# Two of the four copies that free the attention accumulator move from VectorE to ScalarE

## Chip, cores and metric

One Trainium2 chip, 8 cores, one batch element of 8 on each; the cores share nothing. The metric is the device time in microseconds of the slowest core.

## What is computed

One transformer layer, post-norm, for each batch element: a sequence of S = 4096 rows of 1024. Attention with 16 heads of 64 columns from a compressed latent, then a 1024x1024 layer with weights rounded to 4 bits and a rank 16 addition.

```python
c_kv = h @ W_dkv + b_dkv;  c_q = h @ W_dq + b_dq
k = [c_kv @ W_uk | rotary(h @ W_kr)];  v = c_kv @ W_uv
q = [c_q @ W_uq | rotary(c_q @ W_qr)]
attn = softmax(q k^T / 8)                      # 16 heads, 4096 x 4096
x = layernorm(h + (attn @ v) @ W_o + b_o)
w = simulate_quantize_int4(kernel)
out = layernorm(x + x @ w + bias + (x @ a) @ b)
```

## The kernel before, in words

The program is recorded by helpers, one for each kind of operation (`mm` L237, `tr` L243, `act` L249, `tt` L254, `ts` L260, `red` L272, `cp` L276, `recip` L280), so most rows of the profile carry a helper's line and are told apart by their tiles. Every engine works strictly in the order in which its operations were recorded, and waits on counting semaphores: `sPE`, `sAC`, `sDV` count finished operations of TensorE, ScalarE and VectorE, the `q...` ones count DMAs.

Setup (to about 460 us) projects keys and values for the whole sequence into SBUF and prepares the weights. Then comes the attention, in a loop over 8 query tiles (`qt`, 512 queries), 8 head pairs (`p`) and 32 key chunks (`kc`, 128 keys): 64 pairs of 32 chunks. For each chunk:

- `emit_S`: two matmuls, scores of the two heads, into PSUM banks 0 and 1 or 2 and 3, alternating. It waits for the exponential two chunks back.
- `emit_exp`: one ScalarE operation on 128x1024, into one of four buffers (three in `Psb`, one in `wkr_sb`, hence the two names in the profile).
- `emit_pv`, two chunks late: two matmuls of the probabilities with V (`Vsb`), accumulating over the 32 chunks in banks 4 and 5, columns 2048 to 3071 of `PS`. V has a 65th column of ones for each head, so partition 64 of the result holds the softmax denominators and partitions 0 to 63 the sums.

Banks 4 and 5 are there once. So the first PV matmul of a pair (kc = 0) waits until the results of the pair before have been copied out, which `ep_start` does. It is recorded at kc = 1 of the next pair, right behind the last PV matmul of the old one, and issues four copies on VectorE: the two denominator rows to `bcast_sb` (partitions 0 and 32), the two blocks of sums to `oun_sb`. `dnev` and `oune` keep the semaphore values. TensorE's order there is: scores of chunk 1, last PV of the old pair, scores of chunk 2, first PV of the new pair (which waits), scores of chunk 3. ScalarE's is: exponentials of chunks 1, 2, 3.

`ep_chain_gen` carries on while the next pair runs: it writes the denominators to DRAM (`rden`) and reads them back broadcast to all partitions (POOL's queue), takes the reciprocal (L280, 128x512) and multiplies `oun_sb` by it on VectorE (chunk 8), and issues the result to `o_dram` from ScalarE's queue (chunk 13), where the issue waits for the multiply and the exponentials stand behind it.

Beside that, `tail_gen` does the output projection, both layer norms and the last layer of the tile before, a few operations for each chunk from kc = 3 on, on TensorE (bank 7), VectorE (`tA`, `h2`, `x1T`, `st`, `stv`) and a little on ScalarE; `qbuild_gen` builds the next tile's queries. In the first query tile there is no tail work.

Of the kernel before, what the change touches and what calls it, by code (L numbers as in the profile page):

```python
# [9 lines left out]
AF = mybir.ActivationFunctionType  # L10
# [111 lines left out]
def build_program(S):  # L122
# [59 lines left out]
    bcast_sb = sbt("bcast_sb", [128, 512], F32)  # L182
# [16 lines left out]
    PS = nc.alloc_psum_tensor("PS", [128, 4096], F32)  # L199
# [46 lines left out]
    def act(out, in_, func, waits=(), scale=1.0, bias=0.0, extra=()):  # L246
        return S_.ev("scalar",
                     (lambda e, o=out, i=in_, f=func, sc=scale, b=bias:
                      e.activation(o, i, f, scale=sc, bias=b)),  # L249
                     waits, [("sAC", 1)] + list(extra))  # L250
# [24 lines left out]
    def cp(out, in_, waits=(), extra=()):  # L275
        return S_.ev("vector", (lambda e, o=out, i=in_: e.tensor_copy(o, i)),  # L276
                     waits, [("sDV", 1)] + list(extra))
# [21 lines left out]
    for nm, dst in (("ident", ident_sb), ("bdkv", bdkv_sb),  # L299
# [9 lines left out]
                     sem="qCVa")["qCVa"])  # L309
    qcv["dq"] = ("qCVb", dma("gpsimd", wdq_sb,  # L310
                    dr["W_dq"].rearrange("(c p) n -> p c n", p=128),
                    sem="qCVb")["qCVb"])
# [3 lines left out]
                    sem="qCVc")["qCVc"])  # L316
# [10 lines left out]
    for half in range(2):  # L327
# [5 lines left out]
            sem="qWsc")  # L333
# [96 lines left out]
    for s in range(NSP):  # L430
        tau = 512 * s
        tl = dma("sync", cos_sb[:, :], dr["cosT"][:, tau:tau + 512], sem="qT",
                 waits=([("sDV", tbl_free)] if tbl_free else []))
# [4 lines left out]
        for i in range(4):  # L438
            par = i % 2
            w = [("sPE", hload_seen[par])] if hload_seen[par] else []  # L440
            if hload_gate[par]:
# [4 lines left out]
                     waits=w)  # L446
            ldv = ld[qH[par]]
            for c in range(8):
                bk = 2 * par + c // 4
                w2 = []  # L450
                if c == 0:
# [5 lines left out]
                    elif s > 0:  # L457
# [3 lines left out]
                          waits=w2)  # L461
                if c == 3 or c == 7:
                    dst = hT[:, 0:4096].rearrange("p (c t) -> p c t", t=512)[
                        :, 4 * (c // 4):4 * (c // 4) + 4, 128 * i:128 * (i + 1)]
                    e = act(dst, PS[:, 512 * bk:512 * (bk + 1)].rearrange(
                                "p (c t) -> p c t", t=128),
                            AF.Copy, waits=[("sPE", last["sPE"])])
# [5 lines left out]
        for c in range(8):  # L473
            w = []
            if c == 0:
                w = [("sAC", hT_ready)]
# [7 lines left out]
        for c in range(8):  # L484
            mm(PS[:, 2560:3072], wdq_sb[:, 128 * c:128 * (c + 1)],
               hT[:, 512 * c:512 * (c + 1)],
               waits=([qcv["dq"]] if s == 0 and c == 0 else []),
# [3 lines left out]
                 waits=[("sPE", pe_ckv)])  # L491
        ckv_sb = cq_buf[:, 0:512]
        e2 = act(cq_buf[:, 512:1024], PS[:, 2560:3072], AF.Identity, bias=bdq_sb[:, 0:1],
                 waits=[("sPE", pe_cq)] + ([("qCw", cw_cnt)] if cw_cnt else []))
        ckv_ready = e2["sAC"]
        cw = dma("sync", cq_scr[:, tau:tau + 512], cq_buf[:, 512:1024],
                 sem="qCw", waits=[("sAC", e2["sAC"])])
# [3 lines left out]
        for blk, bk in enumerate((6, 7, 0)):  # L501
            for c in range(8):
                w = []
                if c == 0:
                    if blk == 0 and rope_done:
                        w = [("sDV", rope_done)]
                    if blk == 0 and s == 0:
                        w.append(qcv["kr"])
                    if blk == 2:
                        w = [("sAC", ev_done[0])]  # L510
# [7 lines left out]
                 waits=[("sPE", pe_krot - 8)])  # L518
        e5 = act(c0c, PS[:, 0:512], AF.Identity, bias=bkr_sb[:, 2:3],
                 waits=[("sPE", pe_krot)] + ([("qKb", kb_cnt)] if kb_cnt else []))  # L520
        kb1 = dma("sync", rotk_scr[128:256, tau:tau + 512], c0c,
                  sem="qKb", waits=[("sAC", e5["sAC"])])
        e3b = act(c0b_sb[:, :], PS[:, 512 * 6:512 * 7], AF.Identity, bias=bkr_sb[:, 0:1],
                  waits=[("sAC", e4["sAC"])] + ([("qKb", kb_cnt)] if kb_cnt else []))
        e6 = tt(c0b_sb[:, :], c0b_sb[:, :], cos_sb[:, :], ALU.mult,
                waits=[("sAC", e3b["sAC"]), ("qT", tbl_val)])
        e7 = tt(c0s_sb[:, :], c0s_sb[:, :], sin_sb[:, :], ALU.mult,
                waits=[("sDV", e6["sDV"])])
        e8 = tt(c0b_sb[:, :], c0b_sb[:, :], c0s_sb[:, :], ALU.add,
                waits=[("sDV", e7["sDV"])])  # L530
# [3 lines left out]
                  sem="qKb", waits=[("sDV", e8["sDV"])])  # L534
# [4 lines left out]
        for p in range(NP):  # L539
            bk = 1 + p % 2  # L540
            w = []
            if p < 2:
                w = [("sAC", ckv_ready), ("sAC", ev_done[bk])]
                if s == 0:
                    w.append(qcv["kcat"])
            else:
                w = [("sAC", kn_evac[p % 2])]
# [10 lines left out]
        for i in range(4):  # L558
            for half in range(2):
                k = 2 * i + half  # L560
                bk = 3 + k % 2
                if k == 0:
                    w = [("sAC", ev_done[3]), ("sAC", ckv_ready), ("qBB", buv["qBB"])]
# [3 lines left out]
                elif k == 1:  # L567
                    w = [("sAC", e1["sAC"])]
# [120 lines left out]
    denb = [0] * (NGT + 1)  # L689
# [18 lines left out]
    for qt in range(NQT):  # L708
# [3 lines left out]
        def ep_start(PIDX2):  # L712
            lastG = PIDX2 * NKC + NKC - 1
            op_ = 512 * (PIDX2 % 2)
            c1 = cp(bcast_sb[0:1, 0:512], PS[64:65, 2048:2560],
                    waits=[("sPE", denb[lastG])] +
                          ([("sDV", bcf_[PIDX2 - 1])] if PIDX2 > 0 else []))
            c2 = cp(bcast_sb[32:33, 0:512], PS[64:65, 2560:3072])
            dnev[PIDX2] = c2["sDV"]
            cp(oun_sb[0:64, op_:op_ + 512], PS[0:64, 2048:2560],  # L720
               waits=[("qOD", norm_[PIDX2 - 2])] if PIDX2 > 1 else [])
            e = cp(oun_sb[64:128, op_:op_ + 512], PS[0:64, 2560:3072])
            oune[PIDX2] = e["sDV"]
            return e["sDV"], c2["sDV"]

        def ep_chain_gen(PIDX2, e_dv, c2_dv):
            op_ = 512 * (PIDX2 % 2)
            oup = oun_sb[:, op_:op_ + 512]
            Wg = (PIDX2 + 1) * NKC + 1
            def ph(x):  # L730
                return Wg + max(1, (x * NKC) // 32)
            while gctr[0] < ph(2):
                yield "spin"
            wdma0 = dma("gpsimd", rden[PIDX2:PIDX2 + 1, 0:512], bcast_sb[0:1, 0:512],
                        sem="qBC", waits=[("sDV", c2_dv)] +
                        ([("qOD", norm_[PIDX2 - 1])] if PIDX2 > 0 else []))
            wdma = dma("gpsimd", rden[PIDX2:PIDX2 + 1, 512:1024],
                       bcast_sb[32:33, 0:512], sem="qBC")
            rdw[PIDX2] = wdma["qBC"]
            while gctr[0] < ph(4):  # L740
                yield "spin"
            bl = dma("gpsimd", bcast_sb[0:64, :],
                     rden[PIDX2:PIDX2 + 1, 0:512].partition_broadcast(64),
                     sem="qBC", waits=[("qBC", wdma["qBC"])])
            bl2 = dma("gpsimd", bcast_sb[64:128, :],
                      rden[PIDX2:PIDX2 + 1, 512:1024].partition_broadcast(64),
                      sem="qBC")
            while gctr[0] < ph(7):
                yield "spin"
            rr = recip(bcast_sb[:, :], bcast_sb[:, :],  # L750
                       waits=[("qBC", bl2["qBC"]), ("sDV", e_dv)])
            nn = tt(oup, oup, bcast_sb[:, :], ALU.mult,
                    waits=[("sDV", rr["sDV"])])
            bcf_[PIDX2] = nn["sDV"]
            while gctr[0] < ph(12):
                yield "spin"
            od = dma("scalar", o_dram[PIDX2 * 128:(PIDX2 + 1) * 128, :],
                     oup, sem="qOD", waits=[("sDV", nn["sDV"])])
            norm_[PIDX2] = od["qOD"]
# [31 lines left out]
        def emit_pv(p, kc):  # L791
            G = (qt * NP + p) * NKC + kc
            PIDX = qt * NP + p
            p3 = G % 4
            first = (kc == 0)
            lastk = (kc == NKC - 1)
            w = [("sAC", expd[G])]
            if first and PIDX > 0:
                w += [("sDV", oune[PIDX - 1]), ("sDV", dnev[PIDX - 1])]
            mm(PS[0:65, 2048:2560],  # L800
               Vsb[:, 1040 * kc + 65 * (2 * p):1040 * kc + 65 * (2 * p) + 65],
               PSB4[p3][:, 0:512], waits=w,
               start=first, stop=lastk, tp=(0, 0))
            r = mm(PS[0:65, 2560:3072],
                   Vsb[:, 1040 * kc + 65 * (2 * p + 1):1040 * kc + 65 * (2 * p + 1) + 65],
                   PSB4[p3][:, 512:1024],
                   start=first, stop=lastk, tp=(0, 0))
            denb[G] = r["sPE"]
# [337 lines left out]
```

How the kernel before makes its waits and increments, by code:

```python
            def emit(eng):  # L1108
                for fn, waits, incs in S_.events[eng_name]:
                    for s, v in waits:
                        if v > 0:
                            eng.wait_ge(sems[s], v)
                    if fn is None:
                        continue
                    ins = fn(eng)
                    for s, a in incs:
                        ins = ins.then_inc(sems[s], a)
```

## Time and profile before

| | us |
|---|---|
| two runs | 3258.97 and 3322.42, median 3290.7 |
| the profiled execution | 3256.61 |
| its span, slowest core | 3255.0 (cores from 3240.3) |
| TensorE matmul busy | 2555.7 (79%), 10584 matmuls |
| ScalarE busy | 2113.9 (65%) |
| VectorE busy | 1241.5 (38%) |
| GpSimd busy | 230.2 (7%) |
| mean granted TensorE clock, cores | 0.867 to 0.873 |

PE is TensorE, PEld its weight load, ACT is ScalarE, DVE is VectorE, POOL is GpSimd; a q behind a name is that engine's DMA queue. "x2" behind an operation means that so many stand merged in a row of the timeline; the time given is then from the first one's start to the last one's end. In brackets is the idle time before it and what ended it. A granted clock of 1.00 is 2.4 GHz, 0.5 is 1.2 GHz; a value between is a mean over a stretch with both.

### The profile page before, as it was taken

What the parts mean: (1) busy time and instruction counts of PE and PEld (TensorE: products, weight loads), DVE (VectorE), ACT (ScalarE), POOL (GpSimd) and SP (SyncE); (2) the same over time, 40 slices, a digit from 0 to 9 for tenths busy, and PEclk for the clock granted to TensorE, in tenths of its full rate; (3) what the DMA queues carried; (4) which work ended last, traced back from release to release, by engine and by line L of the source; (5) the groups of instructions that cost most, each with busy time, mean ns of one, the idle gap of its engine ahead of it and who ended that gap; (6) DMA issues with size and microseconds to landing.
All of it is one profiled execution on the core that took longest, in us unless ns stands there. A gap on an engine that the chain in (4) does not pass through costs nothing.

```text
span 3255.0 us, 40114 instructions; the slowest of 8 cores (3240.3 to 3255.0 us)
## 1 busy us (share of the span) xinstructions
PE 2555.7 (79%) x10584; PEld 790.4 (24%) x10584; DVE 1241.5 (38%) x1610; ACT 2113.9 (65%) x2353; POOL 230.2 (7%) x393
## 2 busy tenths in 40 slices
PE   3455678899788978888889878898899788988733
PEld 1222212222222222222222222222222222222211
DVE  1456212224443344334432444244433443344344
ACT  1223368888577867786668767886688677877600
POOL 4000000000000010000000000000000000010000
PEclk8666679999898989898889999998899898999866
DMA  6323310001211121212120122012111211121121
GB/s 105 114 94 98 77 57 23 19 24 41 68 56 53 34 81 36 70 34 65 59 67 24 53 66 77 28 43 80 46 58 41 69 54 53 33 77 56 50 91 39
DMA packets 89938, 188.43 MB, mean 58 GB/s; under 512 B 20579, under 2 KB 50532, under 8 KB 89476
## 3 DMA queue, kind: packets, MB, share of 16 engines
q1 hardware_dynamic: 44292, 82.81, 8.5%
q0 software_dynamic: 31616, 77.88, 8.3%
q10 hardware_dynamic: 13824, 25.17, 2.0%
q8 instruction: 107, 1.75, 0.2%
q14 instruction: 99, 0.81, 0.1%
HBM read 144.65 MB, written 51.64 MB: 60 GB/s over the span
## 4 chain that ended last, share of the span: by engine, by line
PE 56%; DVE 17%; issue 10%; ACT 9%; DMA 7%; POOL 1%; DVEq 0%; SPq 0%; ACTq 0%; POOLq 0%
PE PS L237 54%; ACT Psb L249 5%; DVE tA L254 3%; DVE oun_sb L276 3%; ACT wkr_sb L249 2%; DVE bcast_sb L280 2%; PE PS L243 2%; DVE bcast_sb L276 2%; DVE h L254 1%; DVE Qsb L260 1%; DMA rotq_scr<-c0s_sb 1%; DMA x_scr<-tA 1%; DMA h<-h 1%; POOL Vsb L284 1%; DVE Psb L260 1%
## 5 line engine op out<-in xcount | busy, mean ns | idle before, releaser
L249 ACT ACTIVATE Psb<-PS 128x1024 bf16<-128x1024 f32 x1536 | 1514.2, 1042 | 377.7 <-PE PS L237 371.2
L237 PE MATMUL PS<-Psb,Vsb 128*65 128x512 bf16 x3072 | 1026.5, 418 | 184.6 <-DVE oun_sb L276 160.3
L237 PE MATMUL PS<-Qsb,Ksb 64*128 64x512 bf16 x4096 | 842.6, 405 | 68.1 <-ACT Psb L249 45.0
L249 ACT ACTIVATE wkr_sb<-PS 128x1024 bf16<-128x1024 f32 x512 | 534.0, 1043 | 277.3 <-PE PS L237 276.5
L237 PEld LDWEIGHTS PS<-Qsb,Ksb 64*128 64x128 bf16 x4096 | 220.9, 93 | 960.7 <-issue 958.6
L237 PEld LDWEIGHTS PS<-Psb,Vsb 128*65 128x65 bf16 x3072 | 224.0, 114 | 569.4 <-issue 569.4
L237 PE MATMUL PS<-wkr_sb,Vsb 128*65 128x512 bf16 x1024 | 333.9, 409 | 2.6 <-ACT wkr_sb L249 2.6
L254 DVE TENSOR_TENSOR tA<-PS,h 128x512 f32<-128x512 f32 x128 | 88.5, 692 | 585.6 <-PE PS L237 546.4
L280 DVE RECIPROCAL bcast_sb<-bcast_sb 128x512 f32<-128x512 f32 x64 | 214.3, 3349 | 166.7 <-DMA bcast_sb<-rden 166.7
L276 DVE COPY bcast_sb<-PS 1x512 f32<-1x512 f32 x128 | 87.7, 685 | 452.4 <-PE PS L237 449.8
L237 PE MATMUL PS<-wbuf,osb 128*128 128x512 bf16 x512 | 168.4, 415 | 69.6 <-DVE tA L254 53.1
L243 PE MATMUL PS<-ident_sb,h 128*128 128x128 f32 x512 | 104.1, 360 | 113.1 <-DMA h<-h 42.4
L237 PE MATMUL PS<-wbuf,x1T 128*128 128x512 bf16 x512 | 168.0, 422 | 16.0 <-DVE tA L254 13.1
L230 POOL DMA_DIRECT2D rden<-bcast_sb x128 | 63.1, 498 | 1640.9 <-DVE bcast_sb L276 1545.8
L249 ACT ACTIVATE st<-stv,eps_sb 128x1 f32<-128x1 f32 x64 | 19.5, 304 | 190.5 <-DVE stv L254 190.3
L243 PEld LDWEIGHTS PS<-ident_sb,h 128*128 128x128 f32 x512 | 83.5, 189 | 145.5 <-issue 141.8
L260 DVE TENSOR_SCALAR Qsb<-PS,bqc_sb 128x512 bf16<-128x512 f32 x64 | 48.0, 751 | 168.1 <-PE PS L237 168.1
L237 PEld LDWEIGHTS PS<-wkr_sb,Vsb 128*65 128x65 bf16 x1024 | 73.7, 112 | 128.8 <-issue 128.8
L260 DVE TENSOR_SCALAR tA<-tA,stm 128x1024 f32<-128x1024 f32 x64 | 48.2, 753 | 132.7 <-ACT str_ L249 132.7
L249 ACT ACTIVATE Qsb<-PS 128x512 bf16<-128x512 f32 x64 | 37.2, 596 | 90.8 <-PE PS L243 90.5
L237 PE MATMUL PS<-osb,cq_buf 128*128 128x512 bf16 x64 | 36.5, 596 | 72.8 <-DVE Vsb L254 72.5
L276 DVE CAST oun_sb<-PS 64x512 bf16<-64x512 f32 x128 | 87.4, 683 | 4.0
(88 smaller groups left out, 1351.7 us busy)
## 6 DMA issues: line engine op xcount, KB each, us to landing
h<-h SPq DMA_DIRECT2D x64, 512.0 KB, 3.9
wbuf<-wo_p POOLq DMA_DIRECT2D x32, 512.0 KB, 5.8
bcast_sb<-rden POOLq DMA_DIRECT2D x128, 128.0 KB, 2.8
x_scr<-tA POOLq DMA_DIRECT2D x32, 512.0 KB, 3.1
wbuf<-wf_p POOLq DMA_DIRECT2D x32, 512.0 KB, 5.8
h<-x_scr SPq DMA_DIRECT2D x32, 512.0 KB, 3.6
out<-tA ACTq DMA_DIRECT2D x32, 512.0 KB, 2.6
o_dram<-oun_sb ACTq DMA_DIRECT2D x64, 128.0 KB, 1.7
```

Source lines behind the costliest of these rows:

```text
L230: return S_.ev(q, (lambda e, o=out, i=in_: e.dma_start(out=o, in_=i)), waits, [(sem, 16)] + list(extra))
L237: e.matmul(o, l, r, start=s1, stop=s2, tile_position=t, skip_group_check=k)),
L243: (lambda e, o=out, i=in_: e.transpose(o, i, ident_sb[:, :])),
L249: e.activation(o, i, f, scale=sc, bias=b)),
L254: (lambda e, o=out, x=in0, y=in1, p=op: e.tensor_tensor(o, x, y, op=p)),
L260: e.tensor_scalar(o, i, a, None, op0=p)),
L276: return S_.ev("vector", (lambda e, o=out, i=in_: e.tensor_copy(o, i)), waits, [("sDV", 1)] + list(extra))
L280: return S_.ev("vector", (lambda e, o=out, i=in_: e.reciprocal(o, i)), waits, [("sDV", 1)] + list(extra))
L284: return S_.ev("gpsimd", (lambda e, a=ap, x=v: e.memset(a, x)), waits, [("sGP", 1)])
```

## The change

`ep_start` still issues four copies, in another order and on two engines: the two blocks of sums first, on VectorE, the first of them with the wait for the last PV matmul; then the two denominator rows on ScalarE, with the same wait and the one for the multiply of the pair before. The semaphore that `dnev` counts is now `sAC`, and the two places that wait for it follow: the write to `rden` and the first PV matmul.

```diff
         def ep_start(PIDX2):
             lastG = PIDX2 * NKC + NKC - 1
             op_ = 512 * (PIDX2 % 2)
-            c1 = cp(bcast_sb[0:1, 0:512], PS[64:65, 2048:2560],
-                    waits=[("sPE", denb[lastG])] +
-                          ([("sDV", bcf_[PIDX2 - 1])] if PIDX2 > 0 else []))
-            c2 = cp(bcast_sb[32:33, 0:512], PS[64:65, 2560:3072])
-            dnev[PIDX2] = c2["sDV"]
             cp(oun_sb[0:64, op_:op_ + 512], PS[0:64, 2048:2560],
-               waits=[("qOD", norm_[PIDX2 - 2])] if PIDX2 > 1 else [])
+               waits=[("sPE", denb[lastG])] +
+                     ([("qOD", norm_[PIDX2 - 2])] if PIDX2 > 1 else []))
             e = cp(oun_sb[64:128, op_:op_ + 512], PS[0:64, 2560:3072])
             oune[PIDX2] = e["sDV"]
-            return e["sDV"], c2["sDV"]
+            c1 = act(bcast_sb[0:1, 0:512], PS[64:65, 2048:2560], AF.Copy,
+                     waits=[("sPE", denb[lastG])] +
+                           ([("sDV", bcf_[PIDX2 - 1])] if PIDX2 > 0 else []))
+            c2 = act(bcast_sb[32:33, 0:512], PS[64:65, 2560:3072], AF.Copy)
+            dnev[PIDX2] = c2["sAC"]
+            return e["sDV"], c2["sAC"]
...
             wdma0 = dma("gpsimd", rden[PIDX2:PIDX2 + 1, 0:512], bcast_sb[0:1, 0:512],
-                        sem="qBC", waits=[("sDV", c2_dv)] +
+                        sem="qBC", waits=[("sAC", c2_dv)] +
...
             if first and PIDX > 0:
-                w += [("sDV", oune[PIDX - 1]), ("sDV", dnev[PIDX - 1])]
+                w += [("sDV", oune[PIDX - 1]), ("sAC", dnev[PIDX - 1])]
```

ScalarE's order at the first boundary (end of the first pair, first 13 chunks of the second), before. `Psb` and `wkr_sb` are the exponentials' buffers, the last row is the issue of the finished block to DRAM:

```order
L249 ACTIVATE wkr_sb<-PS 128x1024 [waits sPE]
L249 ACTIVATE Psb<-PS 128x1024 [waits sPE] x3
L249 ACTIVATE wkr_sb<-PS 128x1024 [waits sPE]
L249 ACTIVATE Psb<-PS 128x1024 [waits sPE] x3
L249 ACTIVATE wkr_sb<-PS 128x1024 [waits sPE]
L249 ACTIVATE Psb<-PS 128x1024 [waits sPE] x3
L249 ACTIVATE wkr_sb<-PS 128x1024 [waits sPE]
L249 ACTIVATE Psb<-PS 128x1024 [waits sPE] x2
L230 DMA o_dram<-oun_sb 128x512 [waits sDV]
```

The same place now:

```order
L249 ACTIVATE wkr_sb<-PS 128x1024 [waits sPE]
L249 ACTIVATE Psb<-PS 128x1024 [waits sPE] x2
L249 ACTIVATE bcast_sb<-PS 1x512 [waits sPE]
L249 ACTIVATE bcast_sb<-PS 1x512
L249 ACTIVATE Psb<-PS 128x1024 [waits sPE]
L249 ACTIVATE wkr_sb<-PS 128x1024 [waits sPE]
L249 ACTIVATE Psb<-PS 128x1024 [waits sPE] x3
L249 ACTIVATE wkr_sb<-PS 128x1024 [waits sPE]
L249 ACTIVATE Psb<-PS 128x1024 [waits sPE] x3
L249 ACTIVATE wkr_sb<-PS 128x1024 [waits sPE]
L249 ACTIVATE Psb<-PS 128x1024 [waits sPE] x2
L230 DMA o_dram<-oun_sb 128x512 [waits sDV]
```

The two row copies stand between the exponentials of chunks 1 and 2 of the new pair. The issue to `o_dram` keeps its place behind chunk 13.

VectorE's order at the first two boundaries, before:

```order
L260 TENSOR_SCALAR Qsb<-PS,bqc_sb 128x512 [waits sPE] x8
L276 COPY bcast_sb<-PS 1x512 [waits sPE]
L276 COPY bcast_sb<-PS 1x512
L276 CAST oun_sb<-PS 64x512 x2
L280 RECIPROCAL bcast_sb<-bcast_sb 128x512 [waits qBC,sDV]
L254 TENSOR_TENSOR oun_sb<-oun_sb,bcast_sb 128x512 [waits sDV]
L276 COPY bcast_sb<-PS 1x512 [waits sPE,sDV]
```

and now:

```order
L260 TENSOR_SCALAR Qsb<-PS,bqc_sb 128x512 [waits sPE] x8
L276 CAST oun_sb<-PS 64x512 [waits sPE]
L276 CAST oun_sb<-PS 64x512
L280 RECIPROCAL bcast_sb<-bcast_sb 128x512 [waits qBC,sDV]
L254 TENSOR_TENSOR oun_sb<-oun_sb,bcast_sb 128x512 [waits sDV]
L276 CAST oun_sb<-PS 64x512 [waits sPE]
```

The casts follow the wait for TensorE directly. TensorE's order is the same as before, apart from the semaphore that the first PV matmul of a pair waits for; POOL's likewise, for its write to `rden`.

## Rows read from the trace of the kernel before

**Rows 1.** Groups of instructions: busy us, mean ns, idle before, releasers.
```profile
L237 PE MATMUL PS<-Psb,Vsb 128*65 128x512 bf16 x3072 | 1026.5, 418 | 184.6 <-DVE oun_sb L276 160.3 <-DVE st L254 24.2
...
L254 DVE TENSOR_TENSOR tA<-PS,h 128x512 f32<-128x512 f32 x128 | 88.5, 692 | 585.6 <-PE PS L237 546.4 <-DMA x_scr<-tA 39.2
L276 DVE COPY bcast_sb<-PS 1x512 f32<-1x512 f32 x128 | 87.7, 685 | 452.4 <-PE PS L237 449.8
L276 DVE CAST oun_sb<-PS 64x512 bf16<-64x512 f32 x128 | 87.4, 683 | 4.0
```

**Rows 2.** The chain of waits, 496 to 506: start us, us, what.
```profile
497.91 0.68 DVE bcast_sb L276
...
500.75 0.24 issue
501.00 5.02 PE PS L237 x15
```

**Rows 3.** Timeline of the same boundary: start us, us, instruction, [idle before].
```profile
496.48 2.85 ACT L249 ACTIVATE Psb<-PS 128x1024 bf16<-128x1024 f32 x3
496.80 0.39 PE L237 MATMUL PS<-Qsb,Ksb 64*128 64x512 bf16 x2
...
497.67 0.39 PE L237 MATMUL PS<-Qsb,Ksb 64*128 64x512 bf16 x2
...
501.00 0.82 PE L237 MATMUL PS<-Psb,Vsb 128*65 128x512 bf16 x2 [2.94 <-DVE oun_sb L276]
...
502.54 1.02 ACT L249 ACTIVATE wkr_sb<-PS 128x1024 bf16<-128x1024 f32 x1 [3.20 <-PE PS L237]
```

**Rows 4.** Groups of ScalarE, shapes kept apart, columns as in rows 1.
```profile
L249 ACT ACTIVATE Psb<-PS 128x1024 bf16<-128x1024 f32 x1536 | 1514.2, 1042 | 377.7 <-PE PS L237 371.2 <-PE PS L243 3.0 <-issue 0.3
...
L249 ACT ACTIVATE Ksb<-PS,bkc_sb 128x512 bf16<-128x512 f32 x64 | 41.2, 687 | 4.2 <-PE PS L237 3.4
L249 ACT ACTIVATE Qsb<-PS 128x512 bf16<-128x512 f32 x64 | 37.2, 596 | 90.8 <-PE PS L243 90.5
...
L249 ACT ACTIVATE str_<-st 128x1 f32<-128x1 f32 x64 | 13.0, 203 | 6.2 <-ACT st L249 0.4
...
L249 ACT ACT_TABLE_LOAD x1 | 1.3, 1283 | 12.0 <-PE PS L243 12.0
```

**Rows 5.** Timeline at the change from the first to the second query tile.
```profile
704.24 2.85 ACT L249 ACTIVATE Psb<-PS 128x1024 bf16<-128x1024 f32 x3 [1.46 <-PE PS L237]
...
707.77 0.59 PE L237 MATMUL PS<-Psb,Vsb 128*65 128x512 bf16 x2 [1.98 <-DVE oun_sb L276]
```

**Rows 6.** Timeline around the issue of a finished block, first boundary of a query tile.
```profile
1436.42 0.69 DVE L254 TENSOR_TENSOR oun_sb<-oun_sb,bcast_sb 128x512 bf16<-128x512 bf16 x1
...
1438.04 0.33 ACTq L230 DMA_DIRECT2D o_dram<-oun_sb  x1
```

**Rows 7.** Two pairs of equal work: us, busy by engine, PEclk, DMA share, GB/s.
```profile
568.00:600.70 32.70, 29.33 (x131) 8.35 (x129) 6.82 (x7) 29.78 (x33) 2.04 (x4) 1.00 0.05 17
600.70:634.70 34.00, 30.63 (x131) 8.47 (x129) 6.79 (x7) 29.90 (x33) 2.03 (x4) 0.95 0.05 16
```

**Rows 8.** 12 us behind two boundary waits, columns as in rows 7.
```profile
1424.70:1436.70 12.00, 9.06 (x42) 2.57 (x40) 6.37 (x6) 9.24 (x11) 2.03 (x4) 1.00 0.08 24
...
1697.10:1709.10 12.00, 9.07 (x31) 2.04 (x29) 6.28 (x6) 6.87 (x8) 2.04 (x4) 0.72 0.07 24
```

**Rows 9.** Timeline of TensorE behind two shorter waits elsewhere.
```profile
1179.22 0.59 PE L237 MATMUL PS<-wbuf,osb 128*128 128x512 bf16 x2 [1.88 <-DVE tA L254]
...
1180.56 1.06 PE L237 MATMUL PS<-wbuf,osb 128*128 128x512 bf16 x2
...
1534.22 0.38 PE L237 MATMUL PS<-cq_buf,wq_sb 128*128 128x512 bf16 x1 [1.23 <-DVE c0s_sb L260]
...
1534.85 0.62 PE L237 MATMUL PS<-Psb,Vsb 128*65 128x512 bf16 x2
```

**Rows 10.** Who waited for whom, TensorE: us in total, times, longest.
```profile
PE PS L237 <- DVE tA L254: 66.3, 46, 11.2
```

## The prediction

> **What bounds the kernel now.** I read the page first. Its busy times (in the table above) have TensorE at 79% of the span and ScalarE at 65%, so no engine is full, and the question is what the two main engines wait for. The groups of instructions answer it: the matmuls of the probabilities with V lose 184.6 us to waits for VectorE, 160.3 us of it put down to the casts of `oun_sb`, and 24.2 us to an op that stood just behind them [rows 1]. There are 64 head pairs in a core (8 query tiles of 8) and so 63 boundaries; 184.6 / 63 is 2.93 us at each. The chain of waits around one boundary [rows 2] shows how it is made up: the last PV matmul of the old pair ends, then four VectorE copies stand one behind the other from 497.91 to 500.75, and TensorE goes on at 501.00. The timeline there [rows 3] shows both victims. TensorE is idle for 2.94 us. ScalarE, which in this stretch runs its exponentials without a break, runs dry at 499.33 and starts the next at 502.54, after 3.20 us: the scores that it needs are queued behind the waiting PV matmul.
>
> Two regimes matter for what a shorter wait is worth. Between boundaries without tail work ScalarE sets the pace: three exponentials take 2.85 us with the last 1.03 long, so one starts every 0.91 us; the TensorE group of scores and PV starts every 0.87 us (496.80 to 497.67) [rows 3]. With tail work TensorE is the fuller one. In both an earlier first PV matmul moves everything behind it.
>
> **The change, part by part.** VectorE loses 128 copies of a 1x512 row (685 ns each, two and two casts between 497.91 and 500.75, a start every 0.72 us) [rows 1, 2]. It keeps two casts, which now wait for the last PV matmul themselves. They would stand from 497.91 to 499.31, and with the 0.25 us from the end of a cast to the PV matmul (500.75 to 501.00 [rows 2]) TensorE could go on at 499.56.
>
> ScalarE gains the 128 row copies, and its order puts them behind the exponential of chunk 1 and ahead of that of chunk 2. The three exponentials of [rows 3] are chunks 0, 1 and 2, so the first row copy takes the place of the third, at 496.48 + 2 x 0.91 = 498.30. No row shows ScalarE copying a 1x512 row. Its shortest op, 128x1, takes 203 ns; 128x512 out of PSUM takes 596 ns without a bias and 687 ns with one [rows 4]. VectorE's copy of one row costs as much as its cast of 64 rows (685 against 683 ns [rows 1]), so rows don't count but columns do, and I take 596. The next starts after 0.46 us (0.91 less the 0.45 us that separate 1042 from 596). Copies at 498.30 and 498.76, end 499.36, TensorE at 499.61. With 203 ns the casts would decide (499.56), with 687 ns it would be 499.70 to 499.80: between 1.2 and 1.44 us saved, and I take 501.00 - 499.61 = 1.39.
>
> The exponential of chunk 2 moves from 498.30 to 499.22 and ends at 500.25. It is first needed by the scores of chunk 4, which reuse its bank and start a group and more after 499.61 + 0.55 (the scores of chunk 3) + 0.87, at about 501.0, so the 0.92 us on ScalarE are hidden. ScalarE's next one, chunk 3, follows the first PV matmul and moves with it, so the 1.39 us reach the exponentials too. The cover would be gone if ScalarE had no idle stretch there; it stood 3.20 us [rows 3].
>
> At the seven changes of query tile the wait is 1.98 us only, because the exponentials start late there: three from 704.24 [rows 5]. The row copies would start at 706.06 and end at 707.12, TensorE goes on at 707.37 instead of 707.77, and 0.40 us are saved. The sum of the waits is 56 x 1.39 + 7 x 0.40 = 80.6 us. Setup and the last tail are left as they are.
>
> What is late next: the issue of `o_dram<-oun_sb` stands in ScalarE's order ahead of chunk 14 and waits for the multiply by the reciprocals. That multiply ends at 1437.11, the issue is at 1438.04: 0.93 us to spare [rows 6]. The time of the multiply doesn't come from TensorE but from the trip of the denominators through DRAM, whose start stays within 0.1 us, since the second row copy ends at 499.36 instead of 499.31. With 1.39 us less ahead of it, ScalarE would stand 0.5 us, its exponentials behind. This holds at about 15 boundaries, those of the first query tile and the first of each later one, where tail work does not delay ScalarE: 8 us back. The POOL queue only changes which semaphore it waits for.
>
> **The clock.** The granted clock is the second term. In pairs with the same work, 568.0 to 600.7 and 600.7 to 634.7, the time is 32.7 us at 1.00 and 34.0 us at 0.95 [rows 7]. A mean of 0.95 over 34 us means 3.4 us at the lower level, 1.2 GHz, and they cost 1.3 us, 0.4 us for each. The lower level comes right after a boundary wait, but not behind each: two stretches of 12 us behind the same 2.94 us wait have 1.00 and 0.72 [rows 8]. Summed over the stretches of 12 us behind all 63 boundaries I count 243 us at the lower level: 129 at the 40 whose pair number in the tile is 0, 1, 3, 4 or 6, 77 at numbers 2 and 5, where VectorE is late and the wait mostly 3.2 to 3.5 us, and 37 at number 7. The first kind's wait shrinks to 1.55 us, the second's to about 2.0. Is that short enough? A wait of 1.88 us is followed by PV and projection matmuls of double length within a microsecond and a half; one of 1.23 us, by none [rows 9]. 1.55 lies between. I credit three quarters of the 129 and a quarter of the 77: 116 us x 0.4 = 46 us. The bounds are 0 and 243 x 0.4 = 97 us.
>
> [...]
>
> **Sum.** 80.6 + 46 - 8 = 118.6 us. The profiled execution took 3256.6 us (its span 3255.0 and 1.6 around it), so 3138 us. The median of the two runs shown, 3290.7, lies between 3258.97 and 3322.42; the profiled one agrees with the lower. About 2%, 65 us, is what a measurement of this kernel tells from no change.
>
> **Rivals.** (a) The clock doesn't follow: 1.55 us is still long enough beside the other small gaps. Then 80.6 - 8 is left: 3184 us. For it: 1.88 us is followed by double lengths. Chance 0.18.
>
> (b) VectorE's later work gives it back: in the tiles with tail work TensorE also waits 66.3 us for `tA` [rows 10], which stands behind the 3.35 us reciprocal. If these chains keep their place in time at pair numbers 2, 4 and 5, 24 x 1.39 = 33 us and their share of the clock, some 20 us, are lost: 3191 us. Against it: VectorE loses 1.43 us of work ahead of them, and the `tA` additions with which these chains begin wait 546.4 us for TensorE [rows 1], so they come earlier when it does. Chance 0.14.
>
> (c) Slower: switching from Exp to Copy and back reloads ScalarE's function table. A load takes 1283 ns [rows 4]. With one ahead of the row copies and one behind, ScalarE is taken from 498.30 for 2 x 1.28 + 0.92 = 3.48 us; chunk 2's exponential starts at 501.78 and chunk 3's can't before 502.69, where it would have been 502.1 at the full clock (501.00 and 0.55 + 0.32 + 0.25 behind it). From 2.9 us of ScalarE work on the change loses; here 0.6 us x 56 = 33 us: 3290 us. Against it: the one load of the program covers Copy, Identity, Abs, Ln and Exp alike. Chance 0.03. A slow read is a weaker form of it: row copies and casts read the same two PSUM banks at once, in other partitions, which no row of this trace shows. The Trainium skill, page PSUM — Partial Sum Buffer, section on bank collisions, says that two engines may access one bank together as long as they are in different 32-partition quadrants, and row 64 is in another than rows 0 to 63.
>
> (d) The wait doesn't go, because something else stood just behind the copies: 3250 us. The chain [rows 2] names nothing. Chance 0.03.
>
> **Numbers.** The forecast, 3138 us, has 0.62, with a range of its own of 3100 to 3170. The range for 8 in 10 runs from 3085 (the whole clock term) to 3212 (a and b together, nearly). Faster by over 2% is everything below 3191: 0.62, nearly all of (a) and half of (b), 0.86; within 2%: 0.11; slower by over 2%: 0.03, for (c) with a longer load.
>
> **What would show it.** In the profile after: VectorE's chain at a boundary of 1.40 us; row copies on ScalarE of about 600 ns directly behind chunk 1's exponential; the idle time before the first PV matmul at 1.5 to 1.6 us and 63 such waits at some 104 us instead of 184.6; ScalarE idle before `o_dram<-oun_sb` or the exponential behind it at about 15 places; PEclk of 1.00 behind most boundaries and a mean above 0.90 over the run. Row copies of over 1 us, table loads, or an unchanged clock would make the forecast wrong, in that order of weight.

## The result

The changed kernel takes 0.9717 of the time before, with a 95% interval of 0.968 to 0.9753: faster. The median of its 11 runs is 3177.17 us (3160.47 to 3268.92), that of 10 runs of the kernel before 3265.49 us; both hold some runs in which one die ran at a lower clock, which the ratio leaves out, and so do all the ratios below. The profiled execution took 3162.96 us against 3256.61, 93.65 us less; 118.6 us less were forecast.

The groups of instructions of the changed kernel (columns as in [rows 1]):

```profile
L237 PE MATMUL PS<-Psb,Vsb 128*65 128x512 bf16 x3072 | 996.4, 407 | 111.5 <-ACT bcast_sb L249 98.1 <-DVE st L254 13.4
...
L280 DVE RECIPROCAL bcast_sb<-bcast_sb 128x512 f32<-128x512 f32 x64 | 214.4, 3351 | 263.6 <-DMA bcast_sb<-rden 263.6
...
L276 DVE CAST oun_sb<-PS 64x512 bf16<-64x512 f32 x128 | 87.3, 682 | 421.4 <-PE PS L237 419.3
L249 ACT ACTIVATE bcast_sb<-PS 1x512 f32<-1x512 f32 x128 | 75.5, 590 | 4.0 <-PE PS L237 0.9
```

The first line answers to the first of [rows 1]: the waits before a pair's first PV matmul fell from 184.6 to 111.5 us, and most of them (98.1 us) now end with ScalarE's row copy. The row copies take 590 ns each. The table load is in the profile once, as before. VectorE's reciprocal now waits 263.6 us for its DMA, where it waited 166.7 us before.

The timeline of one boundary (the same as in [rows 3]; TensorE's weight loads left out):

```profile
502.42 1.02 ACT L249 ACTIVATE Psb<-PS 128x1024 bf16<-128x1024 f32 x1
502.69 0.39 PE L237 MATMUL PS<-Qsb,Ksb 64*128 64x512 bf16 x2
502.87 1.40 DVE L276 CAST oun_sb<-PS 64x512 bf16<-64x512 f32 x2 [18.69 <-PE PS L237]
503.46 1.20 ACT L249 ACTIVATE bcast_sb<-PS 1x512 f32<-1x512 f32 x2
504.69 1.02 ACT L249 ACTIVATE Psb<-PS 128x1024 bf16<-128x1024 f32 x1
504.81 0.59 PE L237 MATMUL PS<-Psb,Vsb 128*65 128x512 bf16 x2 [1.73 <-ACT bcast_sb L249]
```

The two engines work side by side. VectorE is done at 504.27, ScalarE at 504.66, so ScalarE's pair decides; TensorE starts 0.15 us later, and its wait is 1.73 us where it was 2.94. ScalarE no longer runs dry: its next exponential follows at once.

Behind it the clock still falls at some boundaries and not at others, as the windows view shows for 12 us behind the second and the third (columns as in [rows 7]):

```profile
503.50:515.50 12.00, 10.69 (x42) 2.75 (x42) 4.49 (x4) 10.73 (x13) 2.04 (x4) 0.86 0.08 24
536.00:548.00 12.00, 10.49 (x47) 3.07 (x47) 4.66 (x4) 11.68 (x14) 2.03 (x4) 1.00 0.07 24
```

Counted in the clock records of the traces, the 12 us behind a boundary hold time at the lower level at 409 of the 504 boundaries of the eight cores before (254 us on a core, median) and at 224 of them now (109 us).

To see where the time went, the span is cut where the first copies at a boundary start and where those behind the last pair start. The windows view of the attention phase between them, slowest core, before and after (same columns):

```profile
464.20:3079.90 2615.70, 2252.61 (x9544) 662.91 (x9542) 986.82 (x1233) 1965.75 (x2127) 181.61 (x350) 0.92 0.16 51
```

```profile
471.40:2990.60 2519.20, 2195.80 (x9544) 658.14 (x9542) 899.32 (x1106) 2044.38 (x2253) 182.89 (x350) 0.95 0.17 53
```

VectorE lost 87 us of work, ScalarE gained 79, and the clock rose from 0.92 to 0.95. The same cut on all eight cores gives the medians that are used from here on ("low clock" is the time at the lower level in this phase, "PV wait" the idle time before the PV matmuls in the whole run):

| us, median of 8 cores | setup | attention | last tail | low clock | PV wait |
|---|---|---|---|---|---|
| before | 465.0 | 2609.8 | 175.2 | 421.5 | 187.2 |
| after | 463.7 | 2517.6 | 170.5 | 286.7 | 114.4 |
| difference | -1.3 | -92.2 | -4.7 | -134.8 | -72.8 |

Not all that was saved arrived. TensorE's other waits grew: its scores matmuls wait for exponentials 81.9 us in the attention phase instead of 59.7, and the x @ a matmuls 24.7 us for `x1T` instead of 21.4. By place, 11.8 of the first 22 us are at chunk 19 of pair number 2 of the tiles (15.3 us after, 3.5 before), 4.1 at chunk 16, 2.8 at chunk 14 of pair number 5 and 2.6 at chunk 7 of pair number 6. The place in pair number 2 can be read in the timelines. VectorE before, then after:

```profile
1126.93 3.35 DVE L280 RECIPROCAL bcast_sb<-bcast_sb 128x512 f32<-128x512 f32 x1 [1.18 <-DMA bcast_sb<-rden]
1130.38 0.69 DVE L254 TENSOR_TENSOR oun_sb<-oun_sb,bcast_sb 128x512 bf16<-128x512 bf16 x1
1131.63 0.69 DVE L254 TENSOR_TENSOR tA<-PS,h 128x512 f32<-128x512 f32 x1 [0.56 <-PE PS L237]
```

```profile
1103.87 3.35 DVE L280 RECIPROCAL bcast_sb<-bcast_sb 128x512 f32<-128x512 f32 x1 [3.88 <-DMA bcast_sb<-rden]
1107.32 0.69 DVE L254 TENSOR_TENSOR oun_sb<-oun_sb,bcast_sb 128x512 bf16<-128x512 bf16 x1
1107.93 0.69 DVE L254 TENSOR_TENSOR tA<-PS,h 128x512 f32<-128x512 f32 x1
...
1114.34 0.16 DVE L254 TENSOR_TENSOR stv<-stv,st 128x1 f32<-128x1 f32 x1 [0.17 <-DVE st L254]
```

The addition to `tA` used to wait 0.56 us for TensorE. Now TensorE is earlier, and the addition comes straight behind the multiply: the reciprocal, held by its DMA, sets the pace of the layer norm chain. ScalarE then waits for the end of that chain, and TensorE waits for ScalarE (changed kernel):

```profile
1114.59 0.29 ACT L249 ACTIVATE st<-stv,eps_sb 128x1 f32<-128x1 f32 x1 [1.51 <-DVE stv L254]
...
1116.29 0.39 PE L237 MATMUL PS<-Qsb,Ksb 64*128 64x512 bf16 x2 [2.12 <-ACT Psb L249]
```

Before, that scores matmul waited 0.50 us. Pair number 2 takes 39.8 us where it took 39.1, while the other seven got shorter by 0.9 to 3.0 us.

### The profile page after: what moved, and what is told of

Read it like the earlier page. It is cut to its first block, busy times and chain, and to the rows that moved or that the text cites. A ratio compares the mean times of both kernels' runs of the same rounds, so it can differ in the third digit from the quotient of the medians.

```text
span 3161.4 us, 40178 instructions; the slowest of 8 cores (3145.2 to 3161.4 us)
## 1 busy us (share of the span) xinstructions
PE 2493.6 (79%) x10584; PEld 787.5 (25%) x10584; DVE 1150.9 (36%) x1482; ACT 2193.9 (69%) x2481; POOL 231.4 (7%) x393
## 4 chain that ended last, share of the span: by engine, by line
PE 54%; DVE 14%; ACT 10%; issue 10%; DMA 9%; POOL 1%; DVEq 1%; SPq 0%; ACTq 0%; POOLq 0%
PE PS L237 52%; ACT Psb L249 5%; DVE tA L254 4%; DVE bcast_sb L280 3%; ACT bcast_sb L249 2%; PE PS L243 2%; ACT wkr_sb L249 2%; DVE h L254 2%; DMA bcast_sb<-rden 1%; DMA h<-h 1%; DMA x_scr<-tA 1%; DMA rotq_scr<-c0s_sb 1%; DVE Psb L260 1%; DVE Qsb L260 1%; POOL Vsb L284 1%
## 5 line engine op out<-in xcount | busy, mean ns | idle before, releaser
L237 PE MATMUL PS<-Psb,Vsb 128*65 128x512 bf16 x3072 | 996.4, 407 | 111.5 <-ACT bcast_sb L249 98.1
L237 PE MATMUL PS<-Qsb,Ksb 64*128 64x512 bf16 x4096 | 828.0, 398 | 93.4 <-ACT Psb L249 68.9
L280 DVE RECIPROCAL bcast_sb<-bcast_sb 128x512 f32<-128x512 f32 x64 | 214.4, 3351 | 263.6 <-DMA bcast_sb<-rden 263.6
L237 PE MATMUL PS<-wbuf,x1T 128*128 128x512 bf16 x512 | 158.8, 402 | 14.8 <-DVE tA L254 12.4
L237 PEld LDWEIGHTS PS<-wbuf,osb 128*128 128x128 bf16 x512 | 53.6, 105 | 144.0 <-issue 97.5
```

The lines of the kernel that those rows point to most:

```text
L237: e.matmul(o, l, r, start=s1, stop=s2, tile_position=t, skip_group_check=k)),
L280: return S_.ev("vector", (lambda e, o=out, i=in_: e.reciprocal(o, i)), waits, [("sDV", 1)] + list(extra))
```

## The experiments

**First question: how much of the gain is the shorter wait, how much the clock?** The six or eleven added matmuls below fill TensorE's wait and write a bank that is free then; the results are not used, everything else is computed as before.

e4, on the kernel before:

```diff
             if first and PIDX > 0:
+                for k_ in range(11):
+                    mm(PS[:, 3072:3584], wq_sb[:, 0:128], Vsb[:, 0:512],
+                       waits=[("sDV", qb_state["qb_bank_free"])] if k_ == 0 else [])
                 w += [("sDV", oune[PIDX - 1]), ("sDV", dnev[PIDX - 1])]
```

> The kernel before with 11 such matmuls ahead of each pair's first PV matmul, where it stands 2.94 us; its copies and their wait are as before. This isolates the clock. If the clock term of 0.4 us per us at the lower clock is right, the time at the lower clock in the attention phase falls from 421 us to about 200 and the time by some 80 us, to about 3180, a ratio of 0.975. If only the shorter wait counted in the change, it stays at 3257 within 10 us.

Measured: ratio 0.9681 (0.9637 to 0.9726) to the kernel before. The low clock falls from 421.5 to 146.8 us, the attention phase from 2609.8 to 2517.5. A boundary in its timeline (eight of the eleven stand in the stretch shown):

```profile
505.70 1.89 PE L237 MATMUL PS<-Vsb,wq_sb 128*128 128x512 bf16 x8
506.40 1.40 DVE L276 CAST oun_sb<-PS 64x512 bf16<-64x512 f32 x2
...
508.05 0.59 PE L237 MATMUL PS<-Psb,Vsb 128*65 128x512 bf16 x2 [0.46 <-DVE oun_sb L276]
...
509.14 1.02 ACT L249 ACTIVATE wkr_sb<-PS 128x1024 bf16<-128x1024 f32 x1 [2.76 <-PE PS L237]
```

The PV matmul still comes when the last cast is done, and ScalarE still runs dry for 2.76 us. Only what TensorE does in the wait is different, and behind it the clock:

```profile
505.20:517.20 12.00, 11.54 (x52) 3.59 (x51) 5.36 (x5) 9.24 (x11) 2.03 (x4) 1.00 0.08 24
```

Behind none of the 63 boundaries, on any core, is there time at the lower level left within 12 us; the 146.8 us lie elsewhere. So the clock term is shown, and its price: 92.3 us for 274.7 us at the lower level, 0.34 us for each. The forecast had used 0.4.

e3, the same on the changed kernel with six:

```diff
             if first and PIDX > 0:
+                for k_ in range(6):
+                    mm(PS[:, 3072:3584], wq_sb[:, 0:128], Vsb[:, 0:512],
+                       waits=[("sDV", qb_state["qb_bank_free"])] if k_ == 0 else [])
                 w += [("sDV", oune[PIDX - 1]), ("sAC", dnev[PIDX - 1])]
```

> The changed kernel with 6 more matmuls (128x512, result unused, bank 6) in TensorE's order ahead of each pair's first PV matmul, where TensorE stands 1.73 us; at the full clock they take 1.3 us and fit in. Theory (clock term): the time at the lower clock in the attention phase falls from 287 us (median of the cores) to about 200, and at 0.4 us for each the time falls by about 35 us against the changed kernel. Rival (the lower clock is not tied to these waits or costs nothing, since ScalarE paces): no gain, or a loss of up to 10 us where the six run at the lower clock and end late.

Measured: 0.9588 (0.9551 to 0.9625); low clock 187.7 us, attention phase 2487.2, 30.4 us less than in the changed kernel for 99.0 us, 0.31 us for each. The gain decides for the clock. Behind the second and the third boundary of e3:

```profile
502.70:514.70 12.00, 11.67 (x54) 3.50 (x53) 4.77 (x4) 11.73 (x15) 2.04 (x4) 1.00 0.08 24
535.50:547.50 12.00, 11.56 (x51) 3.30 (x51) 4.04 (x2) 11.72 (x14) 2.03 (x4) 1.00 0.08 23
```

The lower level is gone behind 497 of the 504 boundaries. So the changed kernel's waits of 1.73 us were still long enough to bring the clock down at nearly half of its boundaries.

**Second: is it the second engine or the new order?** e10 puts the row copies back on VectorE, behind the casts:

```diff
-            c1 = act(bcast_sb[0:1, 0:512], PS[64:65, 2048:2560], AF.Copy,
-                     waits=[("sPE", denb[lastG])] +
-                           ([("sDV", bcf_[PIDX2 - 1])] if PIDX2 > 0 else []))
-            c2 = act(bcast_sb[32:33, 0:512], PS[64:65, 2560:3072], AF.Copy)
-            dnev[PIDX2] = c2["sAC"]
+            c1 = cp(bcast_sb[0:1, 0:512], PS[64:65, 2048:2560],
+                    waits=[("sDV", bcf_[PIDX2 - 1])] if PIDX2 > 0 else [])
+            c2 = cp(bcast_sb[32:33, 0:512], PS[64:65, 2560:3072])
+            dnev[PIDX2] = c2["sDV"]
```

> The changed kernel with the two row copies put back on VectorE, behind the casts: the change's order without its second engine. Theory (the gain comes from copies side by side): the wait before a first PV matmul is 2.9 us again, 187 us in all, the lower clock in the attention phase above 400 us, and the time is that of the kernel before or some 5 to 15 us more, since the denominators start 1.4 us later on their way. Rival (the order matters, casts first): part of the 97 us stays.

Measured: 1.0016 (0.9988 to 1.0043), without the 5 to 15 us more that I had thought possible; PV wait 178.3 us, low clock 426.7. The PV matmuls wait for VectorE's row copies again:

```profile
L237 PE MATMUL PS<-Psb,Vsb 128*65 128x512 bf16 x3072 | 1025.7, 418 | 175.7 <-DVE bcast_sb L276 175.6
```

The order alone is worth nothing; the gain is the second engine's. One detail helps below: with the denominators written 1.4 us later and TensorE no earlier, the wait at chunk 19 of pair number 2 is 7.4 us, twice that of the kernel before, with no row copy on ScalarE.

**Third: what took part of the gain back?** The forecast had named one place, the issue of the finished block on ScalarE's queue. e1 moves it from chunk 13 to 19:

```diff
-            while gctr[0] < ph(12):
+            while gctr[0] < ph(18):
                 yield "spin"
             od = dma("scalar", o_dram[PIDX2 * 128:(PIDX2 + 1) * 128, :],
```

> The changed kernel with one number changed: the issue of the finished block on ScalarE's queue moves from chunk 13 to chunk 19. Theory A (the gain was cut because ScalarE stands at this issue for VectorE's multiply): the waits of the scores matmuls for the exponentials fall from 82 us in the attention phase back to about 60, and the time falls by 12 to 22 us against the changed kernel (ratio to it about 0.994). Theory B (the cut comes from the 1.2 us of row copies in ScalarE's stream itself): these waits stay near 80 us and the time within 5 us of the changed kernel.

Measured: 0.9496 (0.9451 to 0.9541), attention phase 2458.2 us, 59 us below the changed kernel. Neither theory holds: the scores' waits did not fall (85.9 us), and the gain is three times what A promised. The edit does two things. `tail_gen` starts when `norm_` is set, and that moved too, so all the tail's work stands at later chunks. e6 separates them; it sets the mark where it was:

```diff
             while gctr[0] < ph(12):
                 yield "spin"
+            norm_[PIDX2] = V("qOD") + 16
+            while gctr[0] < ph(18):
+                yield "spin"
             od = dma("scalar", o_dram[PIDX2 * 128:(PIDX2 + 1) * 128, :],
```

> The changed kernel with the issue of the finished block at chunk 19, as in e1, but with the tail's work recorded at the very chunks where it was. Theory (e1's gain of some 57 us against the changed kernel came from the tail's work starting six chunks later, not from the issue): here only the 4 us of waits at chunk 16 go, so the time is that of the changed kernel, 0 to 8 us below. Rival (the issue itself held everything up): the same gain as e1, some 57 us, ratio to the kernel before 0.950.

Measured: 0.9671 (0.965 to 0.9691), attention phase 2513.1 us, 4.5 below the changed kernel; the wait at chunk 16 is gone. The issue costs 4 to 5 us, which is too little for the ratios of whole runs to tell: their intervals overlap. e8 is the edit of e1 on the kernel before:

```diff
-            while gctr[0] < ph(12):
+            while gctr[0] < ph(18):
```

> The kernel before with the edit of e1 (issue at chunk 19, which also lets the tail's work start six chunks later). If e1's gain is one of the tail's place, it shows without the change too: 40 to 60 us below the kernel before, ratio 0.982 to 0.988, with pair number 3 near 45 us instead of 56. If it belongs to the change (the issue made late by the shorter wait), the time stays within 5 us of the kernel before, which had 0.85 us and more to spare at that issue.

Measured: 0.9734 (0.9681 to 0.9788). The edit, which moves the issue and the tail's work, is worth 84 us in the attention phase (2609.8 to 2526.1) without any of the change, more than I expected; pair number 3 falls from 56.2 to 44.6 us, and pair number 7 takes over work (38.1 to 44.2). Pair number 3, before and then in e8:

```profile
1156.20:1212.90 56.70, 42.18 (x170) 12.21 (x170) 25.39 (x38) 32.66 (x37) 5.81 (x11) 0.85 0.30 92
```

```profile
1141.70:1186.90 45.20, 37.63 (x156) 10.93 (x156) 25.39 (x32) 31.23 (x35) 4.74 (x9) 0.92 0.25 79
```

It holds 14 matmuls less, and the query building in it no longer meets the layer norm: the 30.8 us wait for `stv` is 0 in e1 and e8. So e1's gain is no property of the change. With e6's 4 to 5 us for the issue, the place of the tail's work is what it comes from.

e2 adds to e1 the reciprocal at chunk 11 instead of 8:

```diff
-            while gctr[0] < ph(7):
+            while gctr[0] < ph(10):
                 yield "spin"
             rr = recip(bcast_sb[:, :], bcast_sb[:, :],
```

> As e1, and the reciprocal recorded at chunk 11 in place of chunk 8. Theory C (VectorE, standing 7 us for the denominators' way through DRAM with the tail's work behind it, passes the wait on to TensorE and ScalarE): VectorE's wait for this DMA falls from 264 us to under 120, and the time falls by another 5 to 15 us below e1. Rival: that wait is hidden; then the time is that of e1 within 5 us, or a little more, since the multiply comes later.

Measured: 0.9454 (0.941 to 0.9498), attention phase 13.7 us below e1, as expected in size. Its reason was not: VectorE's wait for this DMA fell only from 215.0 us in e1 to 191.8. e7 has the reciprocal at chunk 11 with the tail unmoved:

```diff
-            while gctr[0] < ph(7):
+            while gctr[0] < ph(10):
...
+            norm_[PIDX2] = V("qOD") + 16
+            while gctr[0] < ph(18):
+                yield "spin"
```

> As e6, and the reciprocal recorded at chunk 11 in place of 8, the tail's work unmoved. Theory (in pair number 2 of a tile the layer norm chain stands on VectorE behind a reciprocal that waits for its DMA, and ScalarE's Ln stands for the chain): the scores' wait at chunk 19 of pair number 2, 15 us in all, falls to under 4, pair number 2 gets shorter by 1.5 us, and the time is 8 to 15 us below e6, unless the later reciprocal meets another chain. Rival (that wait comes from the row copies on ScalarE): it stays at 15 us.

Measured: 0.9515 (0.9491 to 0.9539), attention phase 2456.5, 57 us below e6. And the named wait went the wrong way, from 14.1 to 24.1 us. The timeline of VectorE in pair number 2 shows what stands there:

```profile
1090.00 1.22 DVE L254 TENSOR_TENSOR tA<-tA,bbuf 128x1024 f32<-128x1024 f32 x1 [0.17 <-DVE tA L254]
1091.14 3.34 DVE L280 RECIPROCAL bcast_sb<-bcast_sb 128x512 f32<-128x512 f32 x1
1094.59 0.69 DVE L254 TENSOR_TENSOR oun_sb<-oun_sb,bcast_sb 128x512 bf16<-128x512 bf16 x1
1095.20 1.21 DVE L272 TENSOR_REDUCE st<-tA 128x1 f32<-128x1024 f32 x1
```

At chunk 11 the reciprocal falls into the middle of the layer norm chain, with 4 us of its own, and TensorE's scores waited 3.44 us there. The gain came from elsewhere: the waits at chunk 14 of pair number 5 (32.0 to 4.6 us) and for `x1T` (25.1 to 0), partly replaced by 17.6 us of transposes waiting for `x1T`. So the reciprocal's place had made that wait at chunk 14 too, most of which (29 us) is in the kernel before already. The miss still left two makers for the wait of pair number 2, the reciprocal and the row copies. e11 takes the reciprocal out of the chain's way altogether:

```diff
-            while gctr[0] < ph(7):
+            while gctr[0] < ph(12):
+                yield "spin"
+            norm_[PIDX2] = V("qOD") + 16
+            while gctr[0] < ph(19):
                 yield "spin"
             rr = recip(bcast_sb[:, :], bcast_sb[:, :],
...
-            while gctr[0] < ph(12):
+            while gctr[0] < ph(22):
                 yield "spin"
             od = dma("scalar", o_dram[PIDX2 * 128:(PIDX2 + 1) * 128, :],
```

> The changed kernel with the tail's work unmoved, the reciprocal at chunk 20 and the issue at chunk 23, so that neither stands ahead of the layer norm chain that ends in ScalarE's Ln at about chunk 17 of pair number 2. Theory: the scores' wait at chunk 19 of pair number 2 (15 us after the change, 24 us in e7) falls to under 4 us, since only VectorE's reciprocal made it; pair number 2 falls from 39.8 to about 38 us. Rival (ScalarE's row copies made it): it stays near 15 us. The whole time should be below e6; where it lands depends on which chains the reciprocal meets at chunk 20, and I expect 3110 to 3160.

Measured: 0.9732 (0.9709 to 0.9755). At that place (e11's timeline):

```profile
1130.38 0.39 PE L237 MATMUL PS<-Qsb,Ksb 64*128 64x512 bf16 x2 [0.48 <-ACT Psb L249]
...
1130.91 3.35 DVE L280 RECIPROCAL bcast_sb<-bcast_sb 128x512 f32<-128x512 f32 x1
```

The wait is 3.3 us in all, as in the kernel before (3.5), and pair number 2 takes 37.2 us, with the row copies still on ScalarE. The reciprocal made it. The whole is not faster than the changed kernel (the expected 3110 to 3160 us were missed). With the reciprocal at chunk 20 the scores' waits at chunk 29 of pair numbers 1 and 6 are 43 us, where they were 9, and the wait for `stv` rises from 30.7 to 54.5. That the reciprocal meets other chains there is the likely reason; it was not tested.

**The parts together.** e9 is e2 with the six matmuls of e3:

```diff
+                for k_ in range(6):
+                    mm(PS[:, 3072:3584], wq_sb[:, 0:128], Vsb[:, 0:512],
+                       waits=[("sDV", qb_state["qb_bank_free"])] if k_ == 0 else [])
...
-            while gctr[0] < ph(7):
+            while gctr[0] < ph(10):
...
-            while gctr[0] < ph(12):
+            while gctr[0] < ph(18):
```

> e2 (issue at chunk 19 and reciprocal at chunk 11, tail later) with e3's six filler matmuls. If the clock term adds to the others, some 25 to 30 us below e2: about 3067, ratio to the kernel before 0.938. If ScalarE paces e2 so far that the clock is hidden, less than 10 us below e2.

Measured: 3037.77 us, ratio 0.9298 (0.9278 to 0.9318), faster than both kernels; low clock 99.0 us, attention phase 2395.0, 49.5 us below e2 for 160.4 us less at the lower clock: 0.31 us for each again. More than expected: in e2 the lower clock stood behind 335 of the 504 boundaries, 167 us on a core in the 12 us behind them, where the changed kernel with nearly the same waits (114.4 us in all, 112.5 in e2) has 224 and 109 us. In e9 it is behind none. So the length of the wait does not decide alone.

| median of 8 cores, us | ratio to before | attention | low clock | PV wait |
|---|---|---|---|---|
| before | 1 | 2609.8 | 421.5 | 187.2 |
| after | 0.9717 | 2517.6 | 286.7 | 114.4 |
| e1 issue late, tail late | 0.9496 | 2458.2 | 259.4 | 112.5 |
| e2 and reciprocal late | 0.9454 | 2444.5 | 259.4 | 112.5 |
| e3 filler, after | 0.9588 | 2487.2 | 187.7 | 25.5 |
| e4 filler, before | 0.9681 | 2517.5 | 146.8 | 34.4 |
| e6 issue late | 0.9671 | 2513.1 | 291.8 | 114.4 |
| e7 issue and reciprocal late | 0.9515 | 2456.5 | 252.6 | 114.4 |
| e8 e1's edit, before | 0.9734 | 2526.1 | 332.8 | 175.2 |
| e9 e2 and filler | 0.9298 | 2395.0 | 99.0 | 24.3 |
| e10 order only | 1.0016 | 2612.9 | 426.7 | 178.3 |
| e11 reciprocal at 20 | 0.9732 | 2532.4 | 290.1 | 114.4 |

## Why the prediction was right, and where not

The measured time lies in the range: the median, 3177 us, is 39 us above the forecast of 3138, the profiled execution, 3163 us, 25 us above it. Its steps:

- **The shorter wait, 80.6 us: right in kind, 10% too high.** 72.8 us measured. The step that was off is "the next starts after 0.46 us". The row copies do not overlap as the exponentials do: the first starts when the exponential has ended (503.46), not 0.91 us after its start, and they start 0.61 us apart. So ScalarE was done 1.79 us after the first cast's start and not 1.45, TensorE followed after 0.15 us and not 0.25, and 1.21 us of waiting were saved in place of 1.39. The 596 ns for one of them was right (590).
- **The clock, 46 us: right in sum, by two errors.** The low clock fell by 134.8 us, not 116 (some 145 us less in the 12 us behind the boundaries, 10 to 20 more elsewhere), and one us of it is worth 0.31 to 0.34 us, not 0.4; at 0.33 that is 44.5 us. The price had come from one pair of pairs [rows 7]. e4 shows that this term is real and not a companion of the shorter wait. Rival (a), without it, was wrong, though what spoke for it holds in part: the wait became 1.73 us and not 1.55, and behind it one stretch still has 0.86 where the next has 1.00. The sign "a mean above 0.90 over the run" did not come (0.881 to 0.889), nor could it by the forecast's own 116 us, which lift the mean from 0.87 to 0.89 only.
- **What is late next, 8 us at the issue of the finished block: right in place, too high.** The idle time there is real, 4 to 5 us by e6 and by the waits at chunk 16.
- **Rival (b), priced at 53 us and left out of the forecast: where the sum was wrong.** "They come earlier when TensorE does" holds for most chains, but not for the one in pair number 2. There VectorE had waited for TensorE 0.56 us only, and in the changed kernel the chain hangs on the reciprocal. That hangs on the denominators' way through DRAM and comes 8.6 us after VectorE's first copy at the boundary, where it came 8.1 us after it, while TensorE is 1.2 us earlier. e11 shows the cause. 11.8 us are shown to have gone in this way, and not as waits for `tA`, where (b) looked for them: these are 68.5 us after and 66.3 before. With the other added waits (22.2 us of scores' waits and 3.3 us for `x1T`, less the 4.1 of the issue) it is 21 us; the 2.6 us at pair number 6 were not traced to a cause. Those at pair number 5 (2.8) belong to a wait that the reciprocal makes, since it falls from 32.0 to 4.6 us in e7, but what made it grow was not tested.
- **Rivals (c) and (d): wrong.** One table load, 590 ns a copy, and a wait that fell by 39%. What stood just behind the copies shows in the first line of the groups: 13.4 us end with `st`, where it was 24.2. The read of one bank by both engines at once, which the Trainium skill (page PSUM — Partial Sum Buffer, section on bank collisions) allows for different 32-partition quadrants, shows no slowing: casts of 682 ns beside the row copies against 683 before. In the boundary shown above the two engines are in one bank together for 0.3 us only; where the casts start late, behind other work, for 1.1 us, and the times are the same (changed kernel):

```profile
807.73 1.39 DVE L276 CAST oun_sb<-PS 64x512 bf16<-64x512 f32 x2
807.88 1.20 ACT L249 ACTIVATE bcast_sb<-PS 1x512 f32<-1x512 f32 x2
```

The sum by the measured terms: 72.8 + 44.5 + 4.7 (the last tail) - 25.5 = 96.5 us, against 96.9 in attention and tail. That it closes so well is partly luck, since the price of the clock is known to a tenth only.

The Trainium skill, page TensorE: Matmul & The Clock Gate, section on HAM oscillation, describes a matmul kernel in which the idle gaps between bursts re-throttle the engine, so that each burst starts cold. The trace agrees with the direction: filling the same gap with matmuls took two thirds of the low clock away (421.5 to 146.8 us) and all of it behind the boundaries. But waits of one length are followed by either level here, 2.94 us by 1.00 and by 0.72 [rows 8] and 1.73 us by 1.00 and by 0.86, so a wait's length alone does not forecast the clock.

## What to carry to other kernels

A wait of TensorE can cost twice: its own length, and the clock behind it. Both can be seen in a profile, the second in windows laid behind the wait, and the second can be had alone by giving TensorE something harmless to do while it waits; here that was worth as much as moving the copies. When a wait is shortened, look at each in-order queue for what stands behind an operation whose time is set by a DMA: it does not move with the engine that got faster. And an edit that moves one step by a mark which others read moves them too: e1 looked like a proof of the wrong cause until the mark was left in place.

## What was not expected of the hardware

- ScalarE's exponentials of 128x1024 last 1.02 us and start 0.91 us apart; two copies of 1x512 behind one last 590 ns each and start 0.61 us apart, with no overlap at either end. Whether that lies in the function, the single partition or the 4-byte output was not tried.
- VectorE and ScalarE read the same PSUM bank at once, in other partitions, for up to 1.1 us at a boundary, and took no longer for it: 682 and 590 ns in the mean.
- The clock behind a wait goes by what TensorE does in it: with the wait filled by unused matmuls, the lower level was gone behind all 504 boundaries in e4 and e9 and behind 497 of them in e3; it had been behind 409 before the change and 224 after it.
- Two edits that leave every operation's work unchanged and move only where the tail and the reciprocal stand in the order were worth 59 us on the changed kernel (e1) and 57 us on e6 (e7), each more than half of what the change itself brought.
